# GpSimd's power of mean squares and one inverse deviation computed by ScalarE as logarithm and exponential, and the second group's dt sum five slots later

## The chip, the core and the metric

One core of a Trainium2 chip runs the whole program. The metric is the device time of one execution in microseconds, as the median of several runs. The engines are named as the profile names them: PE is TensorE, DVE is VectorE, ACT is ScalarE, POOL is GpSimd, SP is SyncE. PEld is PE's loading of weights.

## The reference, cut to what matters

Two transformer-like layers run over 2048 tokens of width 512. Layer 0 (a masked linear map and a gated feed-forward) is not touched. Layer 1 is a selective state-space block and then a mixture of low-rank experts. The lines that the change computes in another way are the root mean squares of `ts`, `Bm` and `Cm`, and the inverse deviation of one layer norm; the line that it moves is a part of `dt`:

```python
def _layernorm(x, axis=-1, eps=1e-05):
    m = jnp.mean(x, axis=axis, keepdims=True)
    v = jnp.var(x, axis=axis, keepdims=True)
    return (x - m) / jnp.sqrt(v + eps)
...
        ssm = x @ W_x.T
        ts, Bm, Cm = (ssm[..., :R], ssm[..., R:R + N], ssm[..., R + N:])
        ts = rms_forward(ts)
        Bm = rms_forward(Bm)
        Cm = rms_forward(Cm)
        dt = jax.nn.softplus(ts @ W_dt.T + b_dt)
        A = -jnp.exp(A_log.astype(jnp.float32))
        def step(state, inp):
            dt_t, B_t, C_t, u_t = inp
            dA = jnp.exp(dt_t[..., None] * A)
            state = state * dA + (dt_t * u_t)[..., None] * B_t[:, None, :]
            y = jnp.einsum('bdn,bn->bd', state, C_t)
            return (state, y)
...
    h = _layernorm(x, axis=-1) * (1 + ca) + sa
    x = x + ga * _L1_attn_ref(h, ...)
    h = _layernorm(x, axis=-1) * (1 + cb) + sb
    x = x + gb * _L1_ffn_ref(h, ...)
```

`rms_forward(x)` is x / sqrt(mean(x * x) + 1e-6). The first of the two norms is called a below, the second b. The program computes softplus as relu(v) + ln(1 + exp(-|v|)), so that `dt` is a sum of two tiles; that sum is `dt_add`.

## The kernel before

Layer 1 handles the tokens in 8 chunks of 256. `iteration(i, p, n, ...)` exists once for every engine and has 32 slots (`STEPS`). Slot s is one state index (s % 16) of one group of 512 channels (s // 16, group 0 and group 1) of chunk i. Between the slots' own work, the same 32 slots carry the end of chunk p = i - 1 (output projection, norm b, router, experts) and the start of chunk n = i + 1 (x tiles, convolution, W_x, root mean squares, dt). Each engine's order is written out by hand: `others(...)` holds the work that a slot number brings, and constants such as `WX_AT = 17` and `RA_AT = 17` say at which slot. An engine runs its list in order; semaphores join the lists.

The own work of a slot s:

- POOL writes `dbu` = dtu x B for the slot (`db`, L2097), up to four slots ahead of DVE. For the first four states of a group it also multiplies the finished state by C (`weigh_h`, L2131, three slots behind its own `dbu`).
- ACT writes the decays `ps_a` = exp(dt x A) in two halves (`exps`, L1757); between the halves it saves the last column of the slot before (`carry`, L1777). Its `others(s)` stands behind `exps(s + 1)`.
- DVE runs the recurrence in two halves (`scans`, L2273) and adds the turned state times C into `acc` (`add_state`, L2289), for the twelve states of a group that POOL doesn't weigh.
- PE turns the state (`turn_h`, L1502); for POOL's four it adds them up in PSUM (`add_h`, L1487), which ACT then copies into `acc` (`join_acc`, L1949). DVE's first `add_state` of a group stands behind that join.

Work that the change touches, with its slot:

- `mean_squares` on DVE (slot 20), `rms_pow` on POOL (behind `weigh_h` in slot 22: an addition, L2167, and a power, L2169), `rms_apply` on DVE (slot 22, waits for `rms_done`).
- `inv_std_a` on POOL in slot 24 (four small instructions, L2149 to L2155) for the norm that `normalise` uses in slot 1 of the next iteration. `inv_std_b` on POOL in slot 12 waits for ACT's `variance_b` of slot 9.
- ACT's table sets: "natural_log_exp_and_others" is loaded in slot 23 (L2013) and "exp_and_others" in slot 29 (L2026). `gate_tanh(n, 0)` in slot 20 and `gate_tanh(n, 2)` in slot 30 need tanh.
- `dt_log(n, 0)` on ACT (L1882, slot 26) and `dt_add(n, 0)` on POOL (L2177, slot 29), which waits for it. `dt_add(i, 1)` on POOL in slot 7; behind it on ACT stand `first_decay(i, 1)` in slot 8 (L1771) and `d_u(i, 1)` in slot 10 (L1889), both waiting for `dt_done`.
- `old_state(i, 1)` on POOL in slot 12 (L2107), which needs `first_decay`; `dt_u(i, 1)` and `first_inputs(i, 1)` in slot 15.
- The x path of chunk n, one tile of 128 channels per slot in the slots 6 to 16: PE `x_tile` (L165 to L167), ACT `x_in` (L1823 to L1828), PE `convolve` (L1466), ACT `x_tanh` (L1842), DVE `make_u` (L2303). `x_tile(m)` waits until `make_u(m - 3)` has freed its bank.

Of the kernel before, what the change touches and what calls it, by code (L numbers as in the profile page):

```python
# [28 lines left out]
P = 128  # L29
# [54 lines left out]
JOIN_AT = 5  # L84

# [1025 lines left out]
def layer_1(nc, A, x2_dram, bt_dram, out, W, c, sb, ps, sems):  # L1111
# [49 lines left out]
    nmr = sb("nmr", [P, TT], F32, c)  # L1161
    rl = sb("rl", [P, TT, RA], F32, c)
# [577 lines left out]
    def _(act):  # L1740
# [165 lines left out]

        def router_in(p):
            act.wait_ge(S["ra_mm"], p + 1)
            nc.scalar.activation(rl[:].rearrange("p t w -> p (t w)"), ps_o[:, 0:TT * RA], ACT.Copy, scale=1.0 / WS)\
              .then_inc(S["rl_done"], 1)  # L1910
# [40 lines left out]
        def others(i, p, n, first, s):  # L1951
# [22 lines left out]
            if s == 8:  # L1974
                first_decay(i, 1)
            if s == 10:
                d_u(i, 1)
# [30 lines left out]
            if n is not None:  # L2008
                for m in at_slot(DT_AT, s):
                    if m % 2 == 0:  # L2010
                        dt_abs(n, m)
                if s == 23:
                    nc.scalar.preload_act_table_set("natural_log_exp_and_others")  # L2013
                    if p is not None:
                        router_exp(p)
                        router_share(p)
                if s == 25:
                    dt_decay(n, 0)
                if s == 26:
                    dt_log(n, 0)  # L2020
                if s == 28:
                    first_decay(n, 0)
                    dt_decay(n, 1)
                if s == 29:
                    dt_log(n, 1)
                    nc.scalar.preload_act_table_set("exp_and_others")  # L2026
# [36 lines left out]
        act.wait_ge(S["begun"], 6)  # L2063
# [24 lines left out]
    def _(pool):  # L2088
# [21 lines left out]
        def first_inputs(n, g):  # L2110
# [10 lines left out]
            op.then_inc(S["fold_done"], 1)  # L2121
            pool.wait_ge(S["fold_done"], (n * 2 + g) * 3 + 2)
# [82 lines left out]
        def others(i, p, n, first, s):  # L2205
# [3 lines left out]
            if n is not None and n < LASTC and s == RA_AT + 7:  # L2209
                inv_std_a(n)  # L2210
            if s == 7:
                dt_add(i, 1, first)
            if p is not None and s == 12:
                inv_std_b(p)
            if p is not None and s == RA_AT + 6:
# [3 lines left out]
            if s == 12:  # L2219
# [11 lines left out]
        def iteration(i, p, n, first):  # L2231
            for s in range(STEPS):
# [3 lines left out]
                if n is not None and s == WX_AT + 5:  # L2236
                    rms_pow(n)
# [8 lines left out]
        pool.wait_ge(S["begun"], 6)  # L2246
# [10 lines left out]
    def _(dve):  # L2257
# [196 lines left out]
        nc.vector.memset(root[:], ROOT).then_inc(S["begun"], 1)  # L2454
        diagonals(0)
# [93 lines left out]
```

## Time and profile before

| what | value |
|---|---|
| median of 3 runs (all) | 1514.07 us (1514.06, 1514.89, 1514.07) |
| profiled execution | 1512.44 us |
| its span, first to last instruction | 1510.3 us |
| mean granted TensorE clock | 0.959 |
| busy PE, PEld | 1349.8 us (89%), 1006.2 us (67%) |
| busy DVE | 1213.1 us (80%) |
| busy POOL | 1028.2 us (68%) |
| busy ACT | 952.1 us (63%) |
| chain that ended last | PE 31%, POOL 13%, DVE 12%, ACT 6% of the span |

Layer 0 takes the first third of the span; the loop over chunks runs from about 530 us to the end. In the middle of the loop one iteration takes 118.1 us, and its rows come back in every iteration at the same distances: `weigh_h` of slot 16 starts at 835.10, 953.27, 1071.40 and 1189.57 us. So one iteration, read slot by slot, stands for six. In a timeline row the first number is the start, the second the time to the end of the merged instructions; a bracket gives the engine's idle time before the row and what ended it. Instructions of one engine overlap a little, so the start of the next row, not the end of this one, says when the engine went on.

### The profile page before, as it was taken

The page shows a single profiled execution, that of the slowest core. Times are in us where ns is not written, and L with a number is a line of the kernel's source. Part 1 is how long each engine was busy: PE and PEld are TensorE (multiplying, and loading weights), DVE is VectorE, ACT ScalarE, POOL GpSimd, SP SyncE. Part 2 cuts the span into 40 slices and gives each one's busy share as a digit, 9 for nine tenths or more (in the row PEclk, how much of TensorE's full clock was granted, in tenths as well). Part 3 has the DMA queues.
Part 4 walks back from the last instruction along what each step waited for, and adds up shares of the span by engine and source line. Part 5 has one row for each costly group of instructions (what it writes and reads, how often), then busy time and mean ns, then how long its engine had stood idle before and what let it go on. Part 6 is the DMA issues. An engine that isn't in the chain of part 4 may idle for free.

```text
span 1510.3 us, 25293 instructions
## 1 busy us (share of the span) xinstructions
PE 1349.8 (89%) x8817; PEld 1006.2 (67%) x8817; DVE 1213.1 (80%) x1643; ACT 952.1 (63%) x2617; POOL 1028.2 (68%) x697
## 2 busy tenths in 40 slices
PE   6899999999999959699899899899899999988677
PEld 5566677768776748568668667667766766855543
DVE  5794674556443469999999999999999999999994
ACT  3432343233321577788888897798798888886761
POOL 0353242313212398998998999899899899899870
PEclk9799999999999979899999999999999999999689
DMA  9531222101100200100110110020030020020001
GB/s 331 195 112 37 91 79 84 56 29 36 36 29 15 87 18 1 57 29 15 57 42 1 57 57 1 31 83 1 15 99 1 15 86 14 1 71 29 1 1 42
DMA packets 32388, 77.16 MB, mean 51 GB/s; under 512 B 3667, under 2 KB 4723, under 8 KB 31750
## 3 DMA queue, kind: packets, MB, share of 16 engines
q1 hardware_dynamic: 32262, 75.55, 15.1%
q8 instruction: 70, 1.15, 0.3%
q14 instruction: 56, 0.46, 0.1%
HBM read 66.99 MB, written 8.55 MB: 50 GB/s over the span
## 4 chain that ended last, share of the span: by engine, by line
PE 31%; POOL 13%; DVE 12%; ACT 6%; issue 5%; DVEq 0%; ACTq 0%; POOLq 0%
PE ps_h L1502 10%; DVE h L2273 7%; POOL h L2131 7%; POOL dbu L2097 6%; PE ps_m L1466 4%; DVE acc L2289 3%; ACT ps_a L1757 2%; PE ps_o L1526 2%; PE ps_m L165 2%; PE ps_s L1466 2%; PE ps_m L166 2%; PE ps_m L167 2%; PE ps_m L1426 2%; ACT ab L1889 1%; PE ps_s L165 1%
## 5 line engine op out<-in xcount | busy, mean ns | idle before, releaser
L2273 DVE TENSOR_TENSOR_SCAN h<-ps_a,dbu 128x512 f32<-128x512 f32 x512 | 595.8, 1205 | 21.3 <-ACT ps_a L1757 7.1
L2097 POOL TENSOR_TENSOR dbu<-dtu,b_all 128x1020 f32<-128x1020 f32 x256 | 598.3, 2358 | 14.4 <-DVE h L2273 13.9
L1757 ACT ACTIVATE ps_a<-dt,a_neg 128x256 f32<-128x256 f32 (+1 forms) x1024 | 442.9, 466 | 67.7 <-DVE h L2273 66.6
L1502 PE MATMUL ps_h<-ident,h 128*128 128x128 f32 x1536 | 226.4, 290 | 65.3 <-DVE acc L2289 60.0
L2289 DVE SCALAR_TENSOR_TENSOR acc<-ps_h,c_cur,acc 128x512 f32<-128x512 f32 x384 | 267.9, 737 | 16.9 <-PE ps_h L1502 16.3
L1502 PEld LDWEIGHTS ps_h<-ident,h 128*128 128x128 f32 x1536 | 183.1, 149 | 123.0 <-DVE h L2273 82.4
L724 POOL TENSOR_TENSOR hid_l<-hid,hid_h 128x256 f16<-128x256 f32 (+1 forms) x88 | 77.4, 883 | 155.0 <-ACT hid_h L610 154.8
L2131 POOL TENSOR_TENSOR h<-h,c_all 128x1024 f32<-128x1024 f32 x64 | 151.1, 2362 | 19.2 <-ACT carry L1777 19.2
L602 ACT ACTIVATE sil<-ps_gu 128x256 f32<-128x256 f32 (+1 forms) x88 | 33.9, 385 | 180.6 <-PE ps_gu L167 180.6
L165 PE MATMUL ps_m<-h_h,wi_h 128*128 128x256 f16 x432 | 119.4, 276 | 2.6 <-PEq L155 2.4
L166 PE MATMUL ps_m<-h_l,wi_h 128*128 128x256 f16 x432 | 119.2, 276 | 0.0
L167 PE MATMUL ps_m<-h_h,wi_l 128*128 128x256 f16 x432 | 119.2, 276 | 0.0
L1526 PE MATMUL ps_o<-wo,y 128*128 128x512 f32 x224 | 107.6, 603 | 7.7 <-DVE x L2391 7.7
L1487 PE MATMUL ps_h<-ident,h 128*128 128x128 f32 x512 | 70.4, 283 | 36.9 <-POOL h L2131 36.8
L165 PE MATMUL ps_gu<-h_h,g_h 128*128 128x256 f16 (+1 forms) x352 | 96.6, 274 | 3.8 <-DVE u_l L1016 2.9
L1487 PEld LDWEIGHTS ps_h<-ident,h 128*128 128x128 f32 x512 | 59.9, 145 | 56.0 <-POOL h L2131 43.7
L167 PE MATMUL ps_gu<-h_h,g_l 128*128 128x256 f16 (+1 forms) x352 | 96.5, 274 | 0.0
L166 PE MATMUL ps_gu<-h_l,g_h 128*128 128x256 f16 (+1 forms) x352 | 96.5, 274 | 0.0
L165 PE MATMUL ps_gu<-h_h,u_h 128*128 128x256 f16 (+1 forms) x352 | 96.1, 273 | 0.0
L166 PE MATMUL ps_gu<-h_l,u_h 128*128 128x256 f16 (+1 forms) x352 | 96.1, 273 | 0.0
L167 PE MATMUL ps_gu<-h_h,u_l 128*128 128x256 f16 (+1 forms) x352 | 96.1, 273 | 0.0
L732 POOL COPY x<-x 128x1024 f32<-128x1024 f32 x8 | 8.3, 1037 | 120.5 <-issue 120.5
(406 smaller groups left out, 2876.8 us busy)
## 6 DMA issues: line engine op xcount, KB each, us to landing
b_all<-bt_scratch SPq DMA_DIRECT2D x32, 512.0 KB, 3.9
wm<-in_wmod SPq DMA_DIRECT2D x7, 1024.0 KB, 5.2
wo<-in_wmod SPq DMA_DIRECT2D x5, 1024.0 KB, 8.6
xa<-in_x SPq DMA_DIRECT2D x8, 512.0 KB, 4.5
stage<-in_W_in SPq DMA_DIRECT2D x4, 1024.0 KB
x_scratch<-x SPq DMA_DIRECT2D x8, 512.0 KB, 3.1
c_all<-bt_scratch SPq DMA_DIRECT2D x8, 512.0 KB, 6.0
x<-x_scratch SPq DMA_DIRECT2D x8, 512.0 KB, 3.6
```

The source lines that it names most:

```text
L165: pe.matmul(out, lh, rh, start=(first and k == 0), stop=False)
L166: pe.matmul(out, lh, rl, start=False, stop=False)
L167: mm = pe.matmul(out, ll, rh, start=False, stop=(last and k == n - 1))
L1466: pe.matmul(x_bank(m, first), diag_t[:, m, tap], xw[:, m % 2, tap:tap + CH], start=(tap == 0), stop=False)
L1487: tr = pe.matmul(ps_h[:, t, j * P:(j + 1) * P], h[:, s % RING, j, t * P:(t + 1) * P], W["ident"][:], is_transpose=True, start=(begin and j ...
L1502: tr = pe.transpose(ps_h[:, t, j * P:(j + 1) * P], h[:, s % RING, j, t * P:(t + 1) * P], W["ident"][:])
L1526: mm = pe.matmul(ps_o[:], y[:, k, tok], W["wo"][:, k], start=(k == 0), stop=(k == KI - 1))
L1757: ex = nc.scalar.activation(ps_a[:, j, j % 2:], dt[:, m, j % 2:], ACT.Exp, scale=a_neg[:, m, st:st + 1])
L2097: nc.gpsimd.tensor_tensor(dbu[:, s % AHEAD, :, 1:], dtu[:, :, 1:], b_all[:, st, 1:].unsqueeze(1).to_broadcast([P, DG, CH - 1]), ALU.mult). ...
L2131: nc.gpsimd.tensor_tensor(h[:, s % RING], h[:, s % RING], c_all[:, s % NS, :].unsqueeze(1).to_broadcast([P, DG, CH]), ALU.mult).then_inc(S ...
L2273: nc.vector.tensor_tensor_scan(h[:, s % RING, two].rearrange("p j t -> p (j t)"), ps_a[:, two].rearrange("p j t -> p (j t)"), dbu[:, s % A ...
L2289: op = nc.vector.scalar_tensor_tensor(part, ps_h[:, t], c_t, part, ALU.mult, ALU.add)
```

## The change

- A new one-column tile `rms_eps`, set to 1e-6 by DVE at the start of layer 1.
- For chunks 1 to 7 the root mean squares are computed by ACT in slot 21 (`rms_root`: `Ln` with the bias `rms_eps`, then `Exp` with scale -0.5). The log-and-exp table set is loaded in slot 20 in place of 23. POOL's `rms_pow` stays for chunk 0 alone.
- `inv_std_a` for n = 1 to 6 is done by ACT in slot 24: `Ln`, `Exp`, two copies scaled by a column, one copy scaled by a constant. POOL's stays for n = 0.
- In every iteration but the first, POOL does `dt_add(i, 1)` in slot 12 behind `inv_std_b`, ACT does `first_decay(i, 1)` in slot 10 and `d_u(i, 1)` in slot 12, and POOL does `old_state(i, 1)` in slot 15, inside `first_inputs`.

```diff
+DT_ADD_AT = 12
...
+        def rms_root(n):
+            act.wait_ge(S["ms_done"], n * 2 + 2)
+            nc.scalar.activation(mse[:], msq[:], ACT.Ln, bias=rms_eps[:]).then_inc(S["me_done"], 1)
+            act.wait_ge(S["me_done"], n + 1)
+            nc.scalar.activation(rms[:], mse[:], ACT.Exp, scale=-0.5).then_inc(S["rms_done"], 1)
+
+        def inv_std_a(n):
+
+            at = (n + 1) * TT
+            act.wait_ge(S["aggr_a"], n * TT + TT)
+            nc.scalar.activation(veps[:], var_a[:], ACT.Ln, bias=W["epsilon"][:, 0:1]).then_inc(S["inv_a"], 1)
+            act.wait_ge(S["inv_a"], n * 3 + 1)
+            nc.scalar.activation(rstd[:], veps[:], ACT.Exp, scale=-0.5).then_inc(S["inv_a"], 1)
+            act.wait_ge(S["inv_a"], n * 3 + 2)
+            for t in range(TT):
+                op = nc.scalar.activation(nm[:, t:t + 1], nms_a[:, at + t:at + t + 1], ACT.Copy, scale=rstd[:, t:t + 1])
+            op.then_inc(S["inv_a"], 1)
+            act.wait_ge(S["inv_a"], n * 3 + 3)
+            nc.scalar.activation(nmr[:], nm[:], ACT.Copy, scale=ROOT).then_inc(S["nmr_a"], 1)
...
-            if s == 8:
+            if s == (8 if first else 10):
                 first_decay(i, 1)
-            if s == 10:
+            if s == (10 if first else 12):
                 d_u(i, 1)
...
-                if s == 23:
+                if s == WX_AT + 3:
                     nc.scalar.preload_act_table_set("natural_log_exp_and_others")
-                    if p is not None:
-                        router_exp(p)
-                        router_share(p)
+                if s == WX_AT + 4:
+                    rms_root(n)
+                if n < LASTC and s == RA_AT + 7:
+                    inv_std_a(n)
+                if s == 23 and p is not None:
+                    router_exp(p)
+                    router_share(p)
...
             op.then_inc(S["fold_done"], 1)
+            if g and n:
+                old_state(n, g)
             pool.wait_ge(S["fold_done"], (n * 2 + g) * 3 + 2)
...
-            if n is not None and n < LASTC and s == RA_AT + 7:
-                inv_std_a(n)
-            if s == 7:
-                dt_add(i, 1, first)
             if p is not None and s == 12:
                 inv_std_b(p)
+            if s == (7 if first else DT_ADD_AT):
+                dt_add(i, 1, first)
...
-            if s == 12:
+            if first and s == 12:
                 old_state(i, 1)
...
-                if n is not None and s == WX_AT + 5:
-                    rms_pow(n)
```

ACT's list in an iteration, from its `variance_b` in slot 9 to the x tile of slot 10, before (nms_b and var_b are the variance, xw the copy `x_in`, th the tanh; L1889 is `d_u`):

```order
L1792 ACTIVATE nms_b<-x_sum 128x2 [waits x3_done]
L1797 ACTIVATE h_h,var_b<-x,nms_b 128x512 [waits aggr_b,base_mm,nms_b]
...
L1842 ACTIVATE th<-ps_m 128x256 [waits gate_sg,u_done,conv_pe]
L1757 ACTIVATE ps_a<-dt,a_neg 128x256 [waits scan_half]
...
L1889 ACTIVATE ab<-u,d_vec 128x256 [waits dt_done]
L1889 ACTIVATE ab<-u,d_vec 128x256 x3
L1823 ACTIVATE xw<-hist 128x3 [waits conv_pe,x_mm]
```

The same place now (L1773 is `first_decay`):

```order
L1794 ACTIVATE nms_b<-x_sum 128x2 [waits x3_done]
L1799 ACTIVATE h_h,var_b<-x,nms_b 128x512 [waits aggr_b,base_mm,nms_b]
...
L1844 ACTIVATE th<-ps_m 128x256 [waits gate_sg,u_done,conv_pe]
L1759 ACTIVATE ps_a<-dt,a_neg 128x256 [waits scan_half]
...
L1773 ACTIVATE decay<-a_neg,dt 128x16 [waits dt_done]
L1773 ACTIVATE decay<-a_neg,dt 128x16 x3
L1825 ACTIVATE xw<-hist 128x3 [waits conv_pe,x_mm]
```

`first_decay` stands where `d_u` stood, and it is now the first instruction that waits for `dt_done` of the second group.

POOL's list around slot 12, before (`inv_std_b`, then `old_state`; `dt_add(i, 1)`, L2177, stands five `dbu` earlier):

```order
L2177 TENSOR_TENSOR dt<-relu,ab 128x1024 [waits exp_half,dt_ln]
L2097 TENSOR_TENSOR dbu<-dtu,b_all 128x4x255 [waits scan_half,b_2]
L2097 TENSOR_TENSOR dbu<-dtu,b_all 128x4x255 [waits scan_half] x3
L2097 TENSOR_TENSOR dbu<-dtu,b_all 128x4x255 [waits scan_half,b_3]
L2149 TENSOR_TENSOR veps<-var_b,epsilon 128x2 [waits aggr_b]
L2151 TENSOR_TENSOR rstd<-veps,mhalf 128x2 [waits inv_b]
L2153 TENSOR_TENSOR nm<-nms_b,rstd 128x2 [waits inv_b]
L2155 TENSOR_TENSOR nmr<-nm,root 128x2 [waits inv_b]
L2107 TENSOR_TENSOR decay<-decay,carry 128x64 [waits carry_done,decay0_done]
L2097 TENSOR_TENSOR dbu<-dtu,b_all 128x4x255 [waits scan_half] x3
```

The same place now (L2205 is `dt_add`):

```order
L2123 TENSOR_TENSOR dbu<-dtu,b_all 128x4x255 [waits scan_half,b_3]
L2177 TENSOR_TENSOR veps<-var_b,epsilon 128x2 [waits aggr_b]
L2179 TENSOR_TENSOR rstd<-veps,mhalf 128x2 [waits inv_b]
L2181 TENSOR_TENSOR nm<-nms_b,rstd 128x2 [waits inv_b]
L2183 TENSOR_TENSOR nmr<-nm,root 128x2 [waits inv_b]
L2205 TENSOR_TENSOR dt<-relu,ab 128x1024 [waits exp_half,dt_ln]
L2123 TENSOR_TENSOR dbu<-dtu,b_all 128x4x255 [waits scan_half] x3
```

`dt_add` now stands behind the four instructions of `inv_std_b`, the first of which waits for ACT's variance.

## Rows read from the trace of the kernel before

**Rows 1.** Windows view, slots 7 to 16 of iteration 4; the first line names the columns.

```profile
core 0: us, PE busy (x) PEld busy (x) DVE busy (x) ACT busy (x) POOL busy (x), PEclk, DMA share, GB/s
...
1030.00:1069.00 39.00, 39.00 (x268) 32.44 (x266) 38.16 (x49) 31.72 (x103) 34.77 (x21) 1.00 0.03 9
```

**Rows 2.** Timeline of all engines at the join of group 0, iteration 4.

```profile
1025.25 2.36 POOL L2131 TENSOR_TENSOR h<-h,c_all 128x1024 f32<-128x1024 f32 x1
...
1028.42 1.08 ACT L1949 ACTIVATE acc<-ps_h 128x512 f32<-128x512 f32 x2 [1.16 <-PE ps_h L1487]
...
1029.89 1.41 DVE L2289 SCALAR_TENSOR_TENSOR acc<-ps_h,c_cur,acc 128x512 f32<-128x512 f32 x2 [1.09 <-PE ps_h L1502]
```

**Rows 3.** Timeline of POOL, slots 22 to 29 of iteration 3.

```profile
969.60 0.25 POOL L2167 TENSOR_SCALAR mse<-msq 128x6 f32<-128x6 f32 x1
...
971.25 2.36 POOL L2097 TENSOR_TENSOR dbu<-dtu,b_all 128x1020 f32<-128x1020 f32 x1
...
976.00 0.19 POOL L2149 TENSOR_TENSOR veps<-var_a,epsilon 128x2 f32<-128x2 f32 x1
...
977.47 4.66 POOL L2097 TENSOR_TENSOR dbu<-dtu,b_all 128x1020 f32<-128x1020 f32 x2
...
991.56 2.37 POOL L2177 TENSOR_TENSOR dt<-dt,ab 128x1024 f32<-128x1024 f32 x1
```

**Rows 4.** Groups by line on POOL: count, busy and mean, then idle before.

```profile
L2177 POOL TENSOR_TENSOR dt<-dt,ab 128x1024 f32<-128x1024 f32 x7 | 16.6, 2367 | 4.7 <-ACT ab L1882 4.7
```

**Rows 5.** Timeline of ACT, slots 21 to 26 of iteration 3.

```profile
967.28 0.87 ACT L1757 ACTIVATE ps_a<-dt,a_neg 128x256 f32<-128x256 f32 x2 [0.45 <-DVE h L2273]
...
970.32 1.09 ACT L1949 ACTIVATE acc<-ps_h 128x512 f32<-128x512 f32 x2 [0.89 <-PE ps_h L1487]
...
977.43 1.28 ACT L2013 ACT_TABLE_LOAD   x1
978.73 0.48 ACT L1915 ACTIVATE e<-top 128x1 f32<-128x1 f32 x2
...
980.09 0.85 ACT L1757 ACTIVATE ps_a<-dt,a_neg 128x256 f32<-128x256 f32 x2
...
983.55 0.87 ACT L1757 ACTIVATE ps_a<-dt,a_neg 128x256 f32<-128x256 f32 x2 [0.30 <-DVE h L2273]
984.73 0.21 ACT L1777 ACTIVATE carry<-h 128x4 f32<-128x4 f32 x1 [0.30 <-DVE h L2273]
...
990.34 1.05 ACT L1882 ACTIVATE ab<-ab 128x1024 f32<-128x1024 f32 x1
```

**Rows 6.** Timeline of DVE, slots 22 and 23 of iteration 3.

```profile
971.31 0.22 DVE L2342 TENSOR_TENSOR ssn<-ps_s,rms 128x64 f32<-128x64 f32 x1
...
973.64 2.34 DVE L2273 TENSOR_TENSOR_SCAN h<-ps_a,dbu 128x512 f32<-128x512 f32 x2 [0.51 <-POOL dbu L2097]
```

**Rows 7.** Timeline of all engines, slots 8 to 11 of iteration 4.

```profile
1039.67 0.89 ACT L1771 ACTIVATE decay<-a_neg,dt 128x16 f32<-128x16 f32 x4
...
1045.65 0.20 POOL L2149 TENSOR_TENSOR veps<-var_b,epsilon 128x2 f32<-128x2 f32 x1 [1.84 <-ACT h_l L1797]
...
1047.14 0.35 POOL L2107 TENSOR_TENSOR decay<-decay,carry 128x64 f32<-128x64 f32 x1
...
1048.03 1.70 ACT L1889 ACTIVATE ab<-u,d_vec 128x256 f32<-128x256 f32 x4
...
1050.22 0.37 ACT L1842 ACTIVATE th<-ps_m 128x256 f32<-128x256 f32 x1
1050.63 0.42 DVE L2303 SCALAR_TENSOR_TENSOR u<-th,ps_m 128x256 f32<-128x256 f32 x1 [0.17 <-ACT th L1842]
...
1051.37 0.27 PE L165 MATMUL ps_m<-h_h,wi_h 128*128 128x256 f16 x1
```

**Rows 8.** Timeline of ACT, slot 12 of iteration 4.

```profile
1056.90 0.21 ACT L1823 ACTIVATE xw<-hist 128x3 f32<-128x3 f32 x1 [0.57 <-PE ps_s L167]
...
1058.21 0.60 ACT L1813 ACTIVATE h_h<-ps_o 128x512 f16<-128x512 f32 x1 [0.31 <-PE ps_o L1353]
```

**Rows 9.** The page's costliest groups: POOL's products with C.

```profile
L2131 POOL TENSOR_TENSOR h<-h,c_all 128x1024 f32<-128x1024 f32 x64 | 151.1, 2362 | 19.2 <-ACT carry L1777 19.2
```

More of the change, by code:

```diff
@@ L1161, in layer_1 @@
     nmr = sb("nmr", [P, TT], F32, c)
+    rms_eps = sb("rms_eps", [P, 1], F32, c)
     rl = sb("rl", [P, TT, RA], F32, c)
@@ L2062, in _ @@
         nc.scalar.preload_act_table_set("natural_log_exp_and_others")
-        act.wait_ge(S["begun"], 6)
+        act.wait_ge(S["begun"], 7)
         tsb_in(0)
@@ L2245, in _ @@
         rms_pow(0)
-        pool.wait_ge(S["begun"], 6)
+        pool.wait_ge(S["begun"], 7)
         first_inputs(0, 0)
@@ L2454, in _ @@
         nc.vector.memset(root[:], ROOT).then_inc(S["begun"], 1)
+        nc.vector.memset(rms_eps[:], RMS_EPS).then_inc(S["begun"], 1)
         diagonals(0)
```

## The prediction, made before the changed kernel ran

> **What bounds the kernel now.** I read the busy shares first, then the chain of waits, then one middle iteration slot by slot in the timelines, since the whole change lies in the loop over chunks and the iterations repeat. No engine bounds the whole iteration; three engines take turns. (a) In slots 7 to 16 PE is busy for 39.00 of 39 us and DVE for 38.16, ACT for 31.72 [rows 1]: PE and DVE are both at their limit, and what delays PE there delays the iteration, because slot 16's last column releases POOL's next product with C, and that product always waits for ACT's carry when it waits at all [rows 9]. (b) From the first product with C in slot 19 up to the join of group 1 (slot 21), POOL sets the pace. (c) From slot 29 to the next join of group 0 POOL is again without a gap: from dt_add(n, 0) at 991.56 [rows 3] to the fourth product, which ends at 1025.25 + 2.36 = 1027.6; ACT's join follows at 1028.42 and DVE goes on at 1029.89, after 1.09 us of idling [rows 2]. Between (b) and (c) DVE is the limit and has no waits worth naming. The question for each edit is therefore whether it moves the end of (a), (b) or (c).
>
> **What POOL loses, and whether it helps.** The root goes: from 969.60 to the next dbu at 971.25, 1.65 us. The inverse deviation goes: from 976.00 to 977.47, 1.47 us [rows 3]. Together 3.1 us per iteration, some 20 us over the loop. None of it reaches the end of (c), as I read it: dt_add(n, 0) also waits for ACT's dt_log, which ends at 990.34 + 1.05 = 991.39 [rows 5], 0.17 us before POOL starts at 991.56 [rows 3]. POOL arrives just as ACT delivers. In three of the seven iterations POOL already waits there for ACT, 4.7 us in sum [rows 4]. If POOL comes 3.1 us earlier, it waits 3.1 us for the same logarithm. So this term is zero, and whatever delays dt_log now delays (c).
>
> **What ACT gains in slots 24 to 26.** inv_std_a is five small instructions with three waits on each other. The router's six small ones, also with three such waits, take from 978.73 to 980.09, 1.36 us [rows 5]; for five I take 1.15. ACT has slack before the next halves of its decays: 0.3 us idle before 983.55 and 0.3 before 984.73 [rows 5], and with the overlap of 0.1 us that goes with each, 0.8. So ACT is 0.37 late (0.3 to 0.45), and it runs without a gap from there to dt_log. dt_log ends 0.37 later, at 991.76; POOL starts 0.08 after that, at 991.84, against 991.56: 0.28. In the two early iterations in which POOL already waits it is the full 0.37; in the last of the seven there is no inv_std_a, so nothing. Sum 2 x 0.37 + 4 x 0.29 = **+1.9 us**, bounds 0 (if more slack is found) and 6 x 0.45 = 2.7. The stall that grows is DVE's 1.09 us at the join [rows 2].
>
> **The root on ACT.** The table load comes to slot 20: 1.28 us, the next instruction 1.30 after its start [rows 5]. ACT idles 0.45 us there before 967.28 [rows 5], with the overlap 0.55; slot 22's decays come 0.75 late, and DVE, which is still busy, sees some 0.15 of it. That is covered by what comes next: rms_root stands behind ACT's join, which is at 970.32 and ends at 971.41 [rows 5]. A logarithm and an exponential take some 0.5 us there, so rms_done comes at about 971.85 in place of 971.28, and rms_apply, at 971.31, starts 0.5 late. But behind it scan 23 waited 0.51 us for a dbu [rows 6], and that dbu now comes 1.65 us earlier. The two cancel. Where PE is late with the turned state instead, rms_apply has similar cover. I take +0.1 per iteration, seven iterations, **+0.6 us**; bounds -0.5 x 7 = -3.5 (no delay, and the wait of 0.51 gone) and +0.5 x 7 = +3.5.
>
> The Trainium skill, "ScalarE: Activation LUTs", section "What ACT_TABLE_LOAD costs", counts about 2.66 us for every switch of set, 1283 ns of load and a drain of 1380 ns. The trace agrees with the load and shows no drain behind it: 977.43 to 978.73 [rows 5]. By the page's figure slot 22's decays would be 1.38 us later still, DVE would see it in full, less the cover above, and the sum would be some 6 us larger.
>
> **The moved router part** loses its wait for the load (1.3 us) in slot 23, but ACT waits for DVE in the next slots anyway [rows 5]: nothing.
>
> **dt_add(i, 1) to slot 12.** In slot 7 it stood behind the fourth product, off (c), and POOL then caught up: at slot 12 it idled 1.84 us for ACT's variance [rows 7]. So the old place cost nothing, and leaving it brings nothing. The new place costs. dt_add now starts where old_state started, at 1047.14 [rows 7], and takes 2.37 [rows 4]: dt_done at 1049.51. ACT reaches slot 10's waiting instruction at 1048.03 [rows 7] and now waits 1.55 us, with decays, x tile and tanh queued behind it. It then does first_decay (0.89, the next instruction 0.8 after its start) in place of d_u (1.70, 1.6) [rows 7], which gives back 0.8. The tanh at 1050.22 and DVE's make_u at 1050.63, which already waits 0.17 for it [rows 7], come 0.75 late. The next x tile on PE starts at 1051.37 and needs that make_u, which ended at 1050.63 + 0.42 = 1051.05 [rows 7]; it now ends at 1051.8, so PE starts 0.5 late. From there PE has no gap up to slot 16 [rows 1], so 0.5 stays. d_u costs 1.6 us in slot 12, where ACT idled 0.57 and 0.31 for PE [rows 8]; that puts DVE another 0.25 back, but DVE has a little slack against PE (38.16 of 39 [rows 1]) and gives this back by slot 16. I take 0.5 per iteration, six iterations: **+3.0 us**; bounds 0 and 6 x 1.0 (DVE's 0.75 + 0.25 stay) = 6.0. In the last iteration there are no x tiles; only decays are behind the wait, and I take +0.2 (0 to 1.0). first_decay leaving slot 8 (0.8 us of ACT) brings nothing, as ACT waits for PE's x tile right behind it. old_state moves by three slots on POOL, 0.35 us [rows 7], where POOL is ahead of DVE: nothing. The extra memset runs once, before the loop, some 0.1 us.
>
> **The sum**: 1.9 + 0.6 + 3.0 + 0.2 + 0.1 = +5.8 us. From the profiled execution of 1512.4 us that is 1518.2; the median lies 1.6 above that execution, so I forecast 1514.07 + 5.8 = **1519.9 us**, 0.38% slower.
>
> **Rivals.** (1) *POOL's relief reaches the join* (faster). If dt_log is ready when POOL arrives 3.1 us earlier, the fourth product ends earlier, but DVE can win only its idle 1.09 us there [rows 2]; with six joins that is -6.5, against +3.0 + 0.6 + 0.3 for the rest: -2.6, or 1511.5 us; and if also the 0.51 before scan 23 goes, -6.1, or 1508. It decides at dt_log ending before about 988.5. For it: POOL's rows are gapless there. Against it: 991.39 and the 4.7 us of waits. Chance 0.10. (2) *The delays are swallowed* (within 0.2%): PE or DVE has more slack in slots 10 to 16 than the rows show, so only the 1.9 and some tenths remain: +1 to +3, 1515 to 1517. For it: all slacks here are tenths of a microsecond. Chance 0.25. (3) *Everything adds*: DVE keeps 1.0 per iteration in (a) and 0.5 in (b): 6.0 + 3.5 + 2.7 + 0.3 = +12, 1526. For it: DVE is as full as PE. Chance 0.08. (4) *A drain behind the moved load*: ACT would stand 1.4 us longer in front of slot 22's decays, worth up to 0.9 per iteration after the cover: +6 on top, 1526. This is the mechanism that the page named above would bring; 977.43 to 978.73 speaks against it. Chance 0.02.
>
> **How the numbers follow.** Forecast (+3 to +9 us) 0.55, rivals 0.10, 0.25, 0.08, 0.02. A measurement of this kernel can tell about 0.2%, 3 us, from no change. Faster by more than that: 0.08 of the 0.10. Within: 0.25, the rest of the faster case and the low edge of the forecast, 0.29. Slower: 0.63. The range takes in the forecast, the swallowed case and part of (3): 1513.5 to 1525.
>
> **What would show it.** In the profile after: POOL idle about 3 us before dt_add(n, 0), released by ACT's dt_log; that row 0.3 us later against scan 23 than before. ACT idle about 1.5 us in slot 10 before first_decay, released by POOL's dt; DVE idle 0.9 before the make_u of slot 11; PE's x tile behind it 0.5 late. An iteration of about 119.0 us in place of 118.1. It would be wrong if the wait before make_u is absent, or if DVE's 1.09 at the join of group 0 shrinks.

## The result, and the profile after

The changed kernel takes **1519.0 us** (median of 11 runs, 1512.7 to 1521.6) where the kernel before took 1513.5 us on the same chip (11 runs, 1510.4 to 1515.5). The ratio is 1.0035 with a 95% interval of 1.0022 to 1.0049: slower, by 5.5 us (3.3 to 7.4 by the interval). The forecast was 5.8 us slower, 1519.9 us.

The profiled execution of the changed kernel takes 1515.9 us, with a span of 1513.8 us and a mean granted clock of 0.955. The page confirms that POOL lost work (1028.2 us before, 1010.8 now) and ACT won some (952.1 to 958.6). What POOL was spared came back as idle time in front of one row. Below, the line of the page on the engines, then the group that answers to [rows 4]:

```profile
PE 1348.3 (89%) x8817; PEld 1000.4 (66%) x8817; DVE 1212.9 (80%) x1644; ACT 958.6 (63%) x2661; POOL 1010.8 (67%) x659
...
L2205 POOL TENSOR_TENSOR dt<-dt,ab 128x1024 f32<-128x1024 f32 x7 | 16.6, 2366 | 24.6 <-ACT ab L1884 24.6
```

The idle time before `dt_add(n, 0)` went from 4.7 us to 24.6 us over the seven iterations, all of it released by ACT's logarithm. That is 19.9 us of the roughly 20 us that the root and the inverse deviation had taken from POOL.

**The place of the inverse deviation**, timeline of ACT in iteration 3. It answers to [rows 5]:

```profile
982.61 0.29 ACT L1919 ACTIVATE veps<-var_a,epsilon 128x2 f32<-128x2 f32 x1
982.93 0.20 ACT L1921 ACTIVATE rstd<-veps 128x2 f32<-128x2 f32 x1
983.16 0.48 ACT L1924 ACTIVATE nm<-nms_a,rstd 128x1 f32<-128x1 f32 x2
983.67 0.20 ACT L1927 ACTIVATE nmr<-nm 128x2 f32<-128x2 f32 x1
...
990.27 1.05 ACT L1884 ACTIVATE ab<-ab 128x1024 f32<-128x1024 f32 x1
```

The five instructions take from 982.61 to the next row at 983.78, 1.17 us, and ACT then runs without a gap into the logarithm. POOL and DVE behind it, in the timelines of POOL and DVE (answering to [rows 3] and [rows 2]):

```profile
991.40 2.36 POOL L2205 TENSOR_TENSOR dt<-dt,ab 128x1024 f32<-128x1024 f32 x1 [3.35 <-ACT ab L1884]
```

```profile
1029.73 1.41 DVE L2313 SCALAR_TENSOR_TENSOR acc<-ps_h,c_cur,acc 128x512 f32<-128x512 f32 x2 [1.37 <-PE ps_h L1504]
```

DVE's wait at the join of group 0 is 1.37 us where it was 1.09.

**The place of the dt sum**, timeline of all engines in slots 9 to 11 of iteration 4, answering to [rows 7]:

```profile
1045.48 0.20 POOL L2177 TENSOR_TENSOR veps<-var_b,epsilon 128x2 f32<-128x2 f32 x1 [4.15 <-ACT h_l L1799]
...
1046.98 2.36 POOL L2205 TENSOR_TENSOR dt<-relu,ab 128x1024 f32<-128x1024 f32 x1
...
1049.38 0.90 ACT L1773 ACTIVATE decay<-a_neg,dt 128x16 f32<-128x16 f32 x4 [1.45 <-POOL dt L2205]
...
1050.79 0.37 ACT L1844 ACTIVATE th<-ps_m 128x256 f32<-128x256 f32 x1
...
1051.19 0.42 DVE L2327 SCALAR_TENSOR_TENSOR u<-th,ps_m 128x256 f32<-128x256 f32 x1 [0.88 <-ACT th L1844]
...
1051.66 0.28 PE L166 MATMUL ps_m<-h_h,wi_h 128*128 128x256 f16 x1 [0.29 <-DVE u L2327]
```

From the right to the left: PE waits for DVE's `make_u`, DVE for ACT's tanh, ACT stood 1.45 us for POOL's sum, and POOL started it behind the inverse deviation of norm b.

**An iteration in three stretches.** Single profiled spans are a poor scale here: the first of the starts used below is at 598.07 us in one kernel's profile and at 595.01 in the other's, although layer 0 is the same. I therefore cut every iteration at three rows and use the distances: the start is POOL's first product with C in slot 16, then DVE's scan of slot 23, then DVE's first `add_state` behind the join of group 0, then the next start. An iteration here runs from one start to the next. Before and after, mean of the five middle iterations, in us:

| kernel | start to scan 23 | scan 23 to the join's add | add to next start | iteration | seven iterations |
|---|---|---|---|---|---|
| before | 20.49 | 56.22 | 41.50 | 118.21 | 826.20 |
| after | 20.45 | 56.55 | 42.10 | 119.09 | 831.18 |

The loop is 4.98 us longer: +1.41 us in the second stretch, +3.89 in the third, -0.32 in the first.

### The profile page after: what moved, and what is told of

Read it like the earlier page. It is cut to its first block, busy times and chain, and to the rows that moved or that the text cites. A ratio compares the mean times of both kernels' runs of the same rounds, so it can differ in the third digit from the quotient of the medians.

```text
span 1513.8 us, 25293 instructions
## 1 busy us (share of the span) xinstructions
PE 1348.3 (89%) x8817; PEld 1000.4 (66%) x8817; DVE 1212.9 (80%) x1644; ACT 958.6 (63%) x2661; POOL 1010.8 (67%) x659
## 3 DMA queue, kind: packets, MB, share of 16 engines
q8 instruction: 70, 1.15, 0.3%
## 4 chain that ended last, share of the span: by engine, by line
POOL 32%; PE 18%; issue 7%; DVE 6%; ACT 4%; DVEq 0%; POOLq 0%; ACTq 0%
POOL dbu L2123 17%; POOL h L2159 10%; PE ps_h L1504 5%; DVE h L2297 3%; PE ps_m L1468 3%; POOL dt L2205 2%; DVE acc L2313 2%; PE ps_o L1528 2%; POOL dtu L2231 1%; ACT ps_a L1759 1%; PE ps_m L166 1%; PE ps_s L1468 1%; PE ps_m L167 1%; PE ps_m L168 1%; PE ps_h L1489 1%
```

## Experiments

All whole times below are ratios to the kernel before on the same chip, each with its 95% interval. Where the intervals of two variants overlap, which is often, the stretches of the profiled execution tell them apart. In most of the middle iterations of a kernel these repeat to 0.15 us in the second stretch and 0.02 in the third; an iteration is called disturbed where PE's granted clock fell at the join (the last section shows one). Apart from those, the third stretch was off by 0.1 to 0.2 us in one iteration of three kernels, and the second varied by 0.45 in the kernel with three table loads (below).

### The dt sum: put back, and moved alone

The first kernel is the changed one with the move undone:

```diff
-            if s == (7 if first else DT_ADD_AT):
+            if s == 7:
                 dt_add(i, 1, first)
```

(`first_decay` and `d_u` go back to slots 8 and 10, and `old_state` to slot 12.)

> The changed kernel with the dt sum of the second group back in slot 7, first_decay in 8, d_u in 10, old_state in 12; the root and the inverse deviation stay on ACT. My theory: the moved dt sum costs 0.5 us per iteration through ACT's wait in slot 10, so this kernel loses ACT's 1.45 us idle before first_decay and DVE's 0.88 before make_u in slot 11 (back to 0.17), an iteration takes 118.5 to 118.7 us (119.1 with the whole change, 118.2 before), and the time is some 3 us under the changed kernel and some 2 us over the kernel before. POOL still waits 3.3 us for dt_log, and DVE's stall at the join of group 0 stays at 1.37 us. Rival (the slow-down comes from the work that ACT took over, not from the move): an iteration stays at 119.0 or more.

The second is the kernel before with only that move.

> The kernel before with the dt sum's move alone; the root and the inverse deviation stay on POOL. My theory: DVE idles 0.88 us before make_u in slot 11 as in the changed kernel, DVE's stall at the join of group 0 stays at 1.0 to 1.1 us, an iteration takes 118.7 us, some 3 us over the kernel before in all. Rival 1 (the move costs only together with the fuller ACT): 118.2. Rival 2 (the whole slow-down is the move): 119.1.

Measured: 1.0031 (1.0018 to 1.0045) and 1.0033 (1.0017 to 1.0048). In the undisturbed iterations the third stretch is 41.50 us with the sum back, and 42.10 with the move alone; the second is 56.53 and 56.25. DVE's `make_u` of slot 11, first in the kernel with the sum back, then in the kernel with the move alone:

```profile
1051.84 0.42 DVE L2325 SCALAR_TENSOR_TENSOR u<-th,ps_m 128x256 f32<-128x256 f32 x1 [0.17 <-ACT th L1844]
```

```profile
1054.76 0.42 DVE L2306 SCALAR_TENSOR_TENSOR u<-th,ps_m 128x256 f32<-128x256 f32 x1 [0.88 <-ACT th L1843]
```

So the move alone makes the wait of 0.88 us and the 0.60 us of the third stretch, and nothing in the second. The whole time of the kernel with the sum back did not fall with it. In two of its seven iterations the third stretch was 42.72 and 42.91 us and not 41.50; the last section shows what such an iteration looks like.

### The dt sum ahead of the inverse deviation of norm b

The changed kernel with two calls of slot 12 exchanged on POOL:

```diff
-            if p is not None and s == 12:
-                inv_std_b(p)
             if s == (7 if first else DT_ADD_AT):
                 dt_add(i, 1, first)
+            if p is not None and s == 12:
+                inv_std_b(p)
```

> The changed kernel with the dt sum in front of inv_std_b in slot 12 on POOL: two calls exchanged. The dt sum then runs in POOL's 4.2 us of idling and doesn't wait for the variance. My theory: ACT's 1.45 us idle before first_decay in slot 10 goes, DVE's 0.88 before make_u in slot 11 falls to under 0.2, and an iteration falls from 119.1 to 118.6 us. Rival (the cost is d_u in the fuller slot 12): 119.0 or more, with DVE idle in slot 13 instead.

Measured: 1.0041 (1.0027 to 1.0055); third stretch 41.50, second 56.54. The timeline of POOL, then that of ACT:

```profile
1040.82 2.36 POOL L2205 TENSOR_TENSOR dt<-relu,ab 128x1024 f32<-128x1024 f32 x1
...
1045.02 0.20 POOL L2177 TENSOR_TENSOR veps<-var_b,epsilon 128x2 f32<-128x2 f32 x1 [1.84 <-ACT h_l L1799]
```

```profile
1047.40 0.90 ACT L1773 ACTIVATE decay<-a_neg,dt 128x16 f32<-128x16 f32 x4
```

POOL was ahead of ACT all the time: in the changed kernel it idled 4.15 us for the variance with the sum queued behind. In front of it, the sum starts at 1040.82 and not at 1046.98, ACT has no idle time before the decays, and the 0.60 us are gone. The cost of the move is therefore not its slot but what it stands behind. The timeline of DVE shows by how much DVE was ahead for it: its `make_u` of slot 12 starts 24.36 us after the join's add, where it was 24.81 in the kernel before. By slot 15 that is gone (36.73 us in both), and the third stretch is 41.50 in both. So 0.45 us won by DVE in these slots brought nothing. The loop is still 829.19 us, because in this profile the third stretch of the last iteration is 40.97 us (39.71 in the changed kernel; PE was granted 0.52 from 1384 to 1386 us, at that join) and the first stretch is once 20.98.

### The inverse deviation: two slots earlier, and alone

```diff
-                if n < LASTC and s == RA_AT + 7:
+                if n < LASTC and s == RA_AT + 5:
                     inv_std_a(n)
```

> The changed kernel with ACT's inverse deviation in slot 22 in place of 24. In slot 22 ACT has nothing else and waits over 1.1 us for DVE. My theory: dt_log no longer comes 0.3 us late, so DVE's stall at the join of group 0 falls from 1.37 to about 1.05 us and an iteration from 119.1 to 118.8. Rival (the stall grew because POOL's list changed, not through dt_log): the stall stays at 1.37.

> The kernel before with one part of the change: the inverse deviation of group a on ScalarE in slot 24; the power of the mean squares stays on GpSimd, the dt sum in slot 7. Theory (the 1.4 to 1.7 us of ScalarE's instructions stand ahead of the logarithm of dt): join 0 is 0.3 us later, stretch scan 23 to add 56.5 to 56.6, first and third stretch as before (20.5 and 41.5), an iteration 118.5, the time 2 to 2.5 us above before. Rival (the 0.3 us came with the root on ScalarE or with the earlier table load): stretch 56.2, iteration 118.2.

Measured: 1.0047 (1.0029 to 1.0066) with the inverse deviation in slot 22, and 1.0032 (1.0018 to 1.0045) with it alone, in slot 24. The second stretch: 56.15 and 56.66 us (56.56 where the wait at the join is the usual 1.4). DVE at the join, and POOL ahead of its sum, in the kernel with slot 22:

```profile
1032.53 0.75 DVE L2313 SCALAR_TENSOR_TENSOR acc<-ps_h,c_cur,acc 128x512 f32<-128x512 f32 x1 [1.01 <-PE ps_h L1504]
```

```profile
994.18 2.36 POOL L2205 TENSOR_TENSOR dt<-dt,ab 128x1024 f32<-128x1024 f32 x1 [2.97 <-ACT ab L1884]
```

In slot 22 ACT has room for the five instructions, so the logarithm is on time, the wait at the join is 1.01, and POOL still stands 2.97 us for ACT. That isolates the second term, between 0.33 and 0.40 us per iteration: it comes from ACT's instructions ahead of the logarithm and not from the root.

### The root alone

The kernel before with `rms_pow` replaced by a logarithm and an exponential on ACT, and the table load in slot 20.

> The kernel before with one part of the change: the root of the mean squares as logarithm and exponential on ScalarE. Inverse deviation on GpSimd, the logarithm of dt in slot 26, the dt sum in slot 7. Theory: the apply of the root comes 0.5 us later (18.6 after the start of the iteration, idle about 0.4 for ScalarE) but scan 23 no later than before (20.3 to 20.5), the relief of 1.65 us on GpSimd ends in an idle of 1 to 2 us ahead of its dt sum, since ScalarE's logarithm sets that; idle at join 0 1.0 to 1.1, an iteration 118.2 to 118.4, the time within 2 us of before. Rival (the relief alone brings the join earlier): stretch scan 23 to add at 55.5, an iteration at 117.3. Second rival (the root on ScalarE costs what it is late): iteration at 118.6 to 118.7.

Measured: 1.0000 (0.9985 to 1.0015), iteration 118.11 us, loop 825.24. The apply of the root comes 18.6 us after the start of the iteration and not 18.04, but scan 23 is no later (20.43 us, 20.49 before). POOL's relief ends in front of its sum:

```profile
989.00 2.37 POOL L2201 TENSOR_TENSOR dt<-dt,ab 128x1024 f32<-128x1024 f32 x1 [1.99 <-ACT ab L1884]
```

The second stretch is 56.19 us: the relief alone does not reach the join.

### The other half of the lock: an earlier logarithm

If POOL's relief is worthless because POOL waits for ACT's logarithm, an earlier logarithm should make it worth something. The edit is one number:

```diff
-                if s == 26:
+                if s == 25:
                     dt_log(n, 0)
```

It was made in four kernels that differ in what POOL is relieved of; in all four the dt sum stays in slot 7.

> The kernel before with one edit, the logarithm of dt for group 0 in ScalarE's slot 25 in place of 26. It separates the earlier logarithm from GpSimd's relief. Theory: in the kernel before GpSimd reaches the dt sum with little or no idle (its own work ends about when the logarithm does), so an earlier logarithm alone brings almost nothing: idle at join 0 stays 0.7 to 1.1, iteration 117.9 to 118.3, time within 2 us of before. Rival (the logarithm alone sets the join): idle at join 0 gone, iteration 117.3, as in the kernel with the relief.

> Only the root of the mean squares stays on ScalarE; the inverse deviation is on GpSimd again (slot 24, 1.5 us of GpSimd work), the dt sum in slot 7, the logarithm of dt in ScalarE's slot 25. Theory: GpSimd's relief of 1.65 us an iteration (the power of 128x6) and an earlier logarithm are both there, so GpSimd's sum starts 1.1 us or more earlier than before and the idle at join 0 is again gone or below 0.2 us; stretch scan 23 to add 55.2 to 55.7, iteration 117.2 to 117.8. Rival (it is the 3.1 us of both GpSimd pieces that is needed): about half of the gain, an iteration at 117.9.

> The kernel before with the inverse deviation of group a on ScalarE (slot 22) and the logarithm of dt for group 0 in slot 25; the power of the mean squares stays on GpSimd, the dt sum in slot 7. It is the fourth cell of a square: neither piece off GpSimd with the early logarithm gave 118.20 an iteration, the root off it 117.3, both 117.3. Theory (the join needs about 1.1 us of relief on GpSimd, either piece gives 1.5 or more, and the rest is unused): stretch scan 23 to the add of state 4 55.47, an iteration 117.2 to 117.4, the time 4 to 7 us below before; and the apply of the root never waits for ScalarE (18.04 after the start of the iteration, idle 0). Rival (only the power of 128x6 ahead of the sum counts, since it stands before the inverse deviation in GpSimd's order): stretch 55.9 to 56.3, an iteration at 117.8 or more.

> The changed kernel with three edits: the dt sum of group 1 back in slot 7, ScalarE's inverse deviation in slot 22 in place of 24, and the logarithm of dt for group 0 (dt_log, 1.05 us) in ScalarE's slot 25 in place of 26. Theory (the join of group 0 waits for a chain ScalarE logarithm, GpSimd dt sum, fold, join; GpSimd has stood idle 3.4 us before that sum, so its relief lay unused): the logarithm now comes 2 to 3 us earlier, GpSimd's idle before the sum falls from 3.35 to under 1 us, and DVE's idle before the add of state 4 at join 0 (1.37 in the changed kernel, 1.09 before) is gone. The stretch from scan 23 to that add is 55.2 to 55.5 us (56.2 before, 56.5 after), the next one 41.5, an iteration 117.1 to 117.6 and the time 4 to 7 us below the kernel before. Rival (the join follows TensorE's turned state or DVE's own queue and not GpSimd's chain): the stretch stays at 56.2, an iteration at 118.2, the time within 1 us of before.

| on ACT, with the logarithm in slot 25 | ratio to before | scan 23 to add | iteration | seven iterations |
|---|---|---|---|---|
| neither | 1.0001 (0.9991 to 1.0012) | 56.31 | 118.20 | 825.54 |
| the root | 0.9953 (0.9936 to 0.9970) | 55.47 | 117.31 | 821.42 |
| the inverse deviation (slot 22) | 1.0010 (0.9999 to 1.0022) | 56.40 | 118.39 | 827.49 |
| both (inverse in slot 22) | 0.9970 (0.9961 to 0.9980) | 55.47 | 117.30 | 819.40 |

Neither the early logarithm nor the relief does anything alone. Together they save 0.9 us per iteration, and both such kernels beat the kernel before. POOL and DVE with both pieces on ACT, timelines of the two engines:

```profile
987.65 2.37 POOL L2203 TENSOR_TENSOR dt<-dt,ab 128x1024 f32<-128x1024 f32 x1 [0.44 <-ACT ab L1884]
```

```profile
988.47 2.34 DVE L2295 TENSOR_TENSOR_SCAN h<-ps_a,dbu 128x512 f32<-128x512 f32 x2 [0.29 <-ACT carry L1779]
...
1025.56 2.34 DVE L2295 TENSOR_TENSOR_SCAN h<-ps_a,dbu 128x512 f32<-128x512 f32 x2 [0.27 <-PE ps_h L1489]
1027.81 1.38 DVE L2311 SCALAR_TENSOR_TENSOR acc<-ps_h,c_cur,acc 128x512 f32<-128x512 f32 x2
```

The wait at the join is gone (1.09 us in [rows 2]). The gain is 0.75 and not 1.09 mostly because the early logarithm puts a new wait of 0.29 us on DVE at 988.47. The kernel with neither piece on ACT shows that a shorter wait is not yet a gain. Its POOL and its DVE at the join:

```profile
989.41 2.37 POOL L2177 TENSOR_TENSOR dt<-dt,ab 128x1024 f32<-128x1024 f32 x1
```

```profile
1027.77 1.41 DVE L2289 SCALAR_TENSOR_TENSOR acc<-ps_h,c_cur,acc 128x512 f32<-128x512 f32 x2 [0.70 <-PE ps_h L1502]
```

POOL no longer waits for ACT, being late by its own work; DVE waits 0.70 us and not 1.09, but only because it arrives later itself: the wait of 0.29 us that came with the early logarithm is here too, at 987.64. The stretch is as long as before.

**The third line of the table went against me**: 56.40 us where 55.47 was expected. Its timelines show a flaw of the edit and nothing of the question. First ACT, then POOL:

```profile
979.04 1.28 ACT L1919 ACT_TABLE_LOAD   x1
980.34 0.29 ACT L1919 ACTIVATE veps<-var_a,epsilon 128x2 f32<-128x2 f32 x1
980.65 1.28 ACT L1921 ACT_TABLE_LOAD   x1
981.95 0.20 ACT L1921 ACTIVATE rstd<-veps 128x2 f32<-128x2 f32 x1
...
985.04 1.28 ACT L2035 ACT_TABLE_LOAD   x1
```

```profile
988.00 1.55 POOL L2214 TENSOR_SCALAR wd<-expert,at,w 128x8 f32<-128x8 f32 x4 [1.98 <-issue]
```

The written table load stood in slot 23, behind the inverse deviation in slot 22. The logarithm and the exponential each brought a load of their own, so there were three in the place of one; the router's weights came late, and POOL lost 1.98 us waiting to weigh the experts. (The row names no releaser, "issue"; that it was the weights is read from ACT's timeline, where their last instruction, at 987.32, ends 0.2 us before POOL starts, and from the next run, where the idle time is gone.) The same kernel with the load in slot 20:

```diff
-                if s == 23:
+                if s == WX_AT + 3:
                     nc.scalar.preload_act_table_set("natural_log_exp_and_others")
```

> As the kernel with the inverse deviation alone on ScalarE (slot 22) and the logarithm of dt in slot 25, with one line changed: the one table load of the iteration stands in slot 20, ahead of the inverse deviation, where it stood in slot 23, behind it. In the former the trace showed two further table loads of 1.28 us each iteration inside the inverse deviation, the router's weights late by them, and GpSimd idle for 1.98 us ahead of the experts' weights: what GpSimd was relieved of was lost there. Theory: with the load ahead that idle and the two loads are gone, GpSimd's dt sum starts about 16.2 to 16.6 us after scan 23 (17.8 there), the idle at join 0 is 0 and the stretch scan 23 to the add 55.47, an iteration 117.2 to 117.4, the time 4 to 7 us below before. Rival (it is the power of the mean squares, 1.6 us earlier in GpSimd's order, that must go): the sum stays at 17.8, an iteration at 118.1 or more.

Measured: 0.9975 (0.9964 to 0.9985), iteration 117.32 us, second stretch 55.46. So either piece is enough relief, and the power of the mean squares need not be the one that goes.

### Do the effects add?

The changed kernel with its late dt sum, the inverse deviation in slot 22 and the logarithm in slot 25:

> The changed kernel as it is, its dt sum in slot 12 too, but ScalarE's inverse deviation in slot 22 and the logarithm of dt for group 0 in slot 25. It asks whether the two effects add. Theory: stretch scan 23 to add 55.47 as with the dt sum in slot 7, the stretch from the add to the next iteration 42.1 as in the changed kernel, an iteration 117.9 to 118.1, the time within 2 us of the kernel before. Rival (the late dt sum is covered once the join is early, since ScalarE and GpSimd then run further ahead): third stretch 41.5, an iteration 117.3.

Measured: 0.9983 (0.9969 to 0.9997); stretches 20.32, 55.47 and 42.05 us, iteration 117.84. They add: -0.75 in the second stretch as without the move, +0.55 in the third where the move alone made +0.60, and DVE's wait of 0.88 us before `make_u` is in its place.

## Why the prediction was right

**POOL's relief is worth nothing: right.** The prediction said POOL would wait some 3 us more for the same logarithm; 19.9 us of idle time appeared in that row. The prediction also named the condition on which it would be otherwise (rival 1: the logarithm ending before about 988.5). Made true by the earlier logarithm, it gave the gain in the kernels in which POOL was relieved as well (with only the inverse deviation on ACT, once the table load stood ahead of it); with the relief alone or the logarithm alone there was none.

**The inverse deviation on ACT, +1.9 us: right in mechanism, place and size.** The five instructions took 1.17 us (1.15 taken). POOL's sum comes 0.32 us later against scan 23 and the join's add 0.33, where 0.28 was worked out. Over the first six iterations the stretch grew by 2.04 us. In the last iteration, which has no inverse deviation, it fell from 56.78 to 56.15, which leaves the measured +1.41. That fall is not the change's. In the profile of the kernel before, PE was granted half its clock just ahead of that last join, and DVE waited for it; in the profile of the changed kernel it was not. The windows view of PE before (columns: window, PE busy, granted clock, DMA share, GB/s), then DVE's scan ahead of the join, before and after:

```profile
1378.00:1382.00 4.00, 4.00 (x10) 0.57 0.01 2
```

```profile
1382.64 2.34 DVE L2273 TENSOR_TENSOR_SCAN h<-ps_a,dbu 128x512 f32<-128x512 f32 x2 [1.96 <-PE ps_h L1487]
```

```profile
1383.15 2.34 DVE L2297 TENSOR_TENSOR_SCAN h<-ps_a,dbu 128x512 f32<-128x512 f32 x2 [0.27 <-PE ps_h L1489]
```

The fourteen profiles fall into two kinds there. Six (the kernel before among them) show a grant of 0.50 that begins 5 to 7 us ahead of the last join's add, and a last second stretch of 56.75 to 57.17 us. The other eight show none there; the stretch is 56.14 to 56.29 us in six of them and 55.47 in the two that also have the relief and the earlier logarithm.

**The root on ACT, +0.6: too high, by 0.9 us over the loop.** The delay of 0.5 us at `rms_apply` is there and is covered at scan 23 by the earlier `dbu`, as was written. From the timelines of ACT and DVE, iteration 3:

```profile
970.98 0.30 ACT L1911 ACTIVATE mse<-msq,rms_eps 128x6 f32<-128x6 f32 x1
971.31 0.21 ACT L1913 ACTIVATE rms<-mse 128x6 f32<-128x6 f32 x1
```

```profile
971.55 0.22 DVE L2366 TENSOR_TENSOR ssn<-ps_s,rms 128x64 f32<-128x64 f32 x1 [0.39 <-ACT rms L1913]
```

In four of the seven iterations the first stretch is even shorter than any before, 20.19 to 20.25 us against 20.36 and more. The prediction put the root behind ACT's join, but where PE is late it counted on "similar cover". The join hangs on PE, and in iteration 2 PE was late and the root with it:

```profile
852.67 0.22 DVE L2366 TENSOR_TENSOR ssn<-ps_s,rms 128x64 f32<-128x64 f32 x1 [1.10 <-ACT rms L1913]
```

The windows view of PE ahead of that row (columns: window, PE busy, granted clock, DMA share, GB/s):

```profile
848.00:850.00 2.00, 0.35 (x2) 0.93 0.00 0
850.00:852.00 2.00, 2.00 (x10) 0.50 0.00 0
```

In iteration 3 the same place shows 0.23 us of work from 967 to 969 and a grant of 1.00 throughout. PE had next to no work for 2 us both times. In iteration 2 it was granted 0.50, the lower of its two levels (1.2 GHz), when the work came; in iteration 3 it kept the full 2.4 GHz. The first stretch was 20.97 us against 20.25. The kernel before has such an iteration too (a grant of 0.54 from 733 to 735 us): there `rms_apply` was on time and the stretch was 20.75 against 20.36. So the cover was there in part: in these two iterations the late PE cost some 0.4 us with the root on POOL and 0.7 with it on ACT. How often it strikes differs from profile to profile, and that the mean of all came out level with before is in part luck.

**The dt sum, +3.0 and +0.2: right in every step, 0.1 us too small in size.** ACT waited 1.45 us (1.55 written), and DVE's wait before `make_u` was 0.88 (0.17 + 0.75 = 0.92). Counted from the join's add (1029.89 before, 1029.73 after), PE's x tile behind it started 0.45 us late (0.5 written), and the next x tile, four microseconds on, 0.6 late. Six times 0.59 plus 0.34 in the last iteration make 3.89 in place of 3.2.

The step "PE starts 0.5 late and that 0.5 stays, `d_u` puts DVE another 0.25 back, and DVE gives this back by slot 16" can be followed row by row. DVE's `make_u` of slots 13 and 15 and the first row of PE's x tile of slot 14, iteration 4, before and then after:

```profile
1058.61 0.39 DVE L2303 SCALAR_TENSOR_TENSOR u<-th,ps_m 128x256 f32<-128x256 f32 x1
...
1064.09 0.27 PE L165 MATMUL ps_m<-h_h,wi_h 128*128 128x256 f16 x1
...
1066.62 0.42 DVE L2303 SCALAR_TENSOR_TENSOR u<-th,ps_s 128x256 f32<-128x256 f32 x1 [0.18 <-ACT th L1842]
```

```profile
1059.42 0.42 DVE L2327 SCALAR_TENSOR_TENSOR u<-th,ps_m 128x256 f32<-128x256 f32 x1 [0.18 <-ACT th L1844]
...
1064.52 0.27 PE L166 MATMUL ps_m<-h_h,wi_h 128*128 128x256 f16 x1
...
1067.20 0.39 DVE L2327 SCALAR_TENSOR_TENSOR u<-th,ps_s 128x256 f32<-128x256 f32 x1
```

PE is 0.59 us late at 1064.52 and stays so to the end of the stretch. DVE is 0.72 us late from slot 11 on, 0.97 at 1059.42, 0.74 at 1067.20, where its wait of 0.18 us is gone, and 0.59 by the end. The other iterations of the changed kernel, and the kernel with the move alone, repeat this to some hundredths, apart from one iteration of the latter that was 0.2 us late before the `make_u`. So DVE had slack and PE had none, and the kernel with the sum ahead of the inverse deviation says the same from the other side: DVE came 0.45 us early in slot 12, and the stretch did not get shorter.

The sums of the windows view would mislead here. Over the third stretch, before and then after (columns as in [rows 1]):

```profile
1029.89:1071.39 41.50, 41.50 (x282) 34.57 (x279) 40.65 (x52) 33.94 (x110) 34.88 (x22) 1.00 0.04 14
```

```profile
1029.73:1071.83 42.10, 41.81 (x282) 34.42 (x279) 40.66 (x52) 33.80 (x110) 34.87 (x22) 1.00 0.04 14
```

DVE's idle time grew from 0.85 to 1.44 us, as if it had given nothing back, and PE's only by 0.29, with 0.31 us more counted as work for the same 282 instructions. But between two cuts that both lie 0.6 us further apart the idle time of any engine with unchanged work grows by that 0.6; which engine had slack shows only in the starts of its rows.

**The drain behind the table load** (rival 4) did not appear. The moved load in the changed kernel, timeline of ACT in iteration 3:

```profile
966.44 1.28 ACT L2035 ACT_TABLE_LOAD   x1
967.73 0.22 ACT L1767 ACTIVATE dbu<-fold 128x8 f32<-128x8 f32 x1
```

It is 1.29 us from the load to the next instruction, the load and nothing more, and 1.30 in the experiment with three loads (979.04 to 980.34 and 980.65 to 981.95). By the figure in the Trainium skill, "ScalarE: Activation LUTs", section "What ACT_TABLE_LOAD costs", about 2.66 us would lie there; the measurement decides against that figure.

**The sum.** +2.0 us (the last iteration aside), -0.3 and +3.9 stand for 1.9, 0.6 and 3.2. That makes 5.6; the profile shows a loop 5.0 us longer, because of the 0.6 that the low grant ahead of the last join had cost the kernel before. The medians differ by 5.5, and 5.8 was forecast, with 0.1 for the memset, which no run isolates. That the sum fits so well is partly luck: the root came out 0.9 below its term and the dt sum 0.7 above, and the two cancel.

## What to carry to other kernels

Before an engine is relieved, look at what it waits for next: where its own end and another engine's delivery fall within some tenths of a microsecond, as POOL at 991.56 and ACT at 991.39, each of the two alone brings nothing, and only both moved together do. What is put on the engine that delivers, ahead of the delivery, is paid as far as it goes beyond that engine's slack (1.17 us cost 0.33 here), and it is then worth a look at whether the delivery can go one slot earlier. And a step moved to a later slot costs by what it then stands behind: the same slot 12 cost 0.60 us an iteration behind the instruction that waits, and nothing ahead of it. To tell which of two full engines sets the pace, delay both and see which one catches up: row by row from a common start, not by sums of busy and idle time.

## What the runs showed of the hardware

PE's granted clock fell now and then right behind a short stretch with little work at a join, in some iterations and not in others with the same rows. The kernel with the inverse deviation alone shows it at the join of iteration 4 and, one iteration later, the same pattern without it. Timeline of DVE at the first, then the windows view of PE there (columns: window, PE busy, granted clock, DMA share, GB/s), then the windows one iteration later:

```profile
1029.89 1.54 DVE L2311 SCALAR_TENSOR_TENSOR acc<-ps_h,c_cur,acc 128x512 f32<-128x512 f32 x2 [1.69 <-PE ps_h L1504]
```

```profile
1026.00:1028.00 2.00, 0.62 (x6) 1.00 0.00 0
1028.00:1030.00 2.00, 1.60 (x11) 0.77 0.00 0
1030.00:1032.00 2.00, 2.00 (x5) 0.50 0.00 0
```

```profile
1145.80:1147.80 2.00, 0.53 (x5) 1.00 0.00 0
1147.80:1149.80 2.00, 1.60 (x15) 1.00 0.00 0
```

Where it happens, DVE waits 1.18 us once more three rows on. In three of the four cases the join's wait is 1.69 to 1.80 us in place of 1.4, and the third stretch is 1.2 to 1.4 us longer (42.72, 42.79 and 42.91 us against 41.50). It struck two of the seven joins of group 0 in the kernel with the sum back, one in that with the inverse deviation alone and the last one in that with the sum ahead of the inverse deviation (there with a wait of 1.14 us and a third stretch of 40.97). It struck none in the profiles of before and after. All four cases lie in the four kernels that have ACT's inverse deviation in slot 24 and so a longer wait at the join: four of their 28 joins, none of the 70 in the other ten kernels. That points to the longer wait making it likelier, so that the 0.33 us cost more than they measure. But the changed kernel, one of the four, shows none, one of the four cases stands at a join whose wait was not longer, and there is one profile of each kernel: it stays open.

Open too is why the whole times of the kernels with parts of the change do not follow their loops. The kernel with slot 22 has a loop 2.9 us shorter than the changed kernel's (828.31 against 831.18) and a ratio of 1.0047 against 1.0035; the intervals overlap, and layer 0 alone moves the start of the loop between 595.0 and 603.5 us from one profile to the next. The terms above therefore rest on distances within the loop, and the whole times only say this: with the logarithm in slot 26, the kernels with the late dt sum or the inverse deviation in slot 24 are slower than before, and the one with the root alone is not; those with the relief and the early logarithm are faster, the one with three table loads excepted.
